# GpSimd splits the bias rows only after VectorE has made the one-hot tables of the edges

## The chip, the cores and the metric

The kernel runs on one core of one Trainium2 chip. The metric is the device time of one execution in microseconds (us). A core has five engines with queues of their own: TensorE (PE in the profile, PEld for its weight loads), VectorE (DVE), ScalarE (ACT), GpSimd (POOL) and SyncE (SP, which here issues most of the DMAs). They are ordered by semaphores alone.

## What is computed

Four graph layers over 64 nodes with 768 features and 1024 edges of 3 relations, each followed by a residual and a layer norm:

```python
x = layernorm(x + L0(x))   # 2 x (relational GCN, relu, gate over 64 queries)
x = layernorm(x + L1(x))   # GCN
x = layernorm(x + L2(x))   # 2 x relational graph attention
x = layernorm(x + L3(x))   # 2 x GCN

def rgcn(x, W_rel, W_root, bias, src, dst, etype):
    xr = einsum('ni,rio->rno', x, W_rel)
    msg = xr[etype, src]
    out = x @ W_root + bias
    for r in range(3):
        m = etype == r
        s = segment_sum(where(m[:, None], msg, 0.0), dst, n)
        c = segment_sum(m.astype(x.dtype), dst, n)
        out = out + s / maximum(c, 1.0)[:, None]
    return out
```

Nine bias vectors of 768 floats are inputs. They are given to the kernel as float32.

## The kernel before

**Edges as matrices.** The kernel never gathers along edges. It makes one-hot tables of the edges (128 partitions with 8 edges each): `hot_src` with 3 x 64 columns an edge (relation and source node) at L771, and `hot_dst` with 64 columns, written twice side by side, by the two instructions of L775. Eight bf16 matmuls (L1284) multiply the tables into a count matrix `M` of 64 x 192 in PSUM. From `M` VectorE makes degrees and the normalised adjacency (L782 to L801), PE turns it (L1295), and every graph layer multiplies with it.

**Biases.** A bias is added by a matmul of its own (L1123, L1160) into the PSUM bank of a layer. To keep float32 exactness with bf16 operands, each bias is split into three bf16 parts, stacked in the tile `biases` (3 x 32 rows, of which 9 each are used). GpSimd does this once: it clears `biases` (L579), waits for the nine bias rows from HBM, and then casts, subtracts and casts again (L581 to L586), each instruction waiting for the one before through `link`. The last two raise `biases_split`, and PE waits for 2 of it in front of the first layer's bias matmul.

**Start of the kernel.** The first 40 us prepare the gate of layer 0: `Wg` and the query embeddings arrive, PE turns them block by block (L1079), and ScalarE and VectorE copy each turned group from PSUM to the tiles `W` (L457). Groups are numbered, a group has three 128 x 128 blocks, and `group_on_act` says who copies which: of groups 8 to 13 VectorE has 11 and 13. Then PE multiplies the queries with the turned weights in eight units (`query_unit`, L1253). Each half of a unit is six records of L1253 in the trace. The order on each engine is written out by hand. On VectorE it is: group copies up to 7, the cast of the edge lists (L766, L768), L771, the two L775, group copies 11 and 13, the copy of unit 0 (L761), a further group, then the chain L782 to L801. On PE: transposes, half a unit, the transposes of groups 8 to 13, the other half of unit 0, then a wait until groups 8 to 13 are copied out (`wait_groups_out(pe, G_Q1)`), half of unit 1, the transposes of the next queries, a wait for the three tables, the counts, and so on to the mix of the nodes (L1269) and the first graph layer (L1105, 96 matmuls against four weight matrices of 2.3 MB).

**GpSimd.** Its stream makes constants for the first 10 us, then does the bias split, and is idle until the first gate. There it copies parts of the node terms into `stack` (L595) and makes 20 of the 32 products `prod = pre * qn` of that gate (L609); VectorE makes the other 12 (L905).

**Semaphores that matter here.** `hot_ready` counts the three tables (1 each from L771 and the two L775); before, only PE waits for it. `bias_loaded` counts 16 for each of nine row transfers, issued by ScalarE's queue. `pool_chain` orders GpSimd's own instructions. `blocks_ready` tells PE that the adjacency can be turned. The weight transfers are issued in order by SyncE: rel1_0 and rel1_1 at once, rel1_2 after the transposes of groups up to 13, root1 after the transposes of `Wg_h`.

Of the kernel before, what the change touches and what calls it, by code (L numbers as in the profile page):

```python
# [19 lines left out]
def gnn_kernel(nc: bass.Bass, a, out):  # L20
# [24 lines left out]
    SLOT = {key: s for key, s, _ in PLAN}  # L45
    PARTS = {key: n for key, _, n in PLAN}

    with ExitStack() as ctx:
# [3 lines left out]
        def sem(name):  # L52
            return ctx.enter_context(nc.semaphore(name))
# [119 lines left out]


        loaded = {key: [sem(f"{key}_{c}_loaded") for c in range(n)] for key, _, n in PLAN}
        Wg_q_rows = [sem(f"Wg_q_rows_{i}") for i in range(JC)]
        warm_ready = sem("warm_ready")
# [13 lines left out]
        hot_ready = sem("hot_ready")  # L191
# [345 lines left out]
        def _(pool):  # L537
            made = [0]

            def link(ins):  # L540

                made[0] += 1
                ins.then_inc(pool_chain, 1)
                pool.wait_ge(pool_chain, made[0])
# [32 lines left out]

            nb = len(BIASES)
            link(nc.gpsimd.memset(biases[:, :], 0.0))  # L579
            pool.wait_ge(bias_loaded, 16 * nb)  # L580
            link(nc.gpsimd.tensor_copy(biases[0:nb, :], bias[:, :]))  # L581
            link(nc.gpsimd.tensor_tensor(bias[:, :], bias[:, :], biases[0:nb, :], ALU.subtract))
# [1141 lines left out]
```

## Time and profile before

| | |
|---|---|
| median of 3 runs | 270.37 us (269.51 to 270.51) |
| profiled execution, its time | 270.35 us |
| its span, first to last instruction | 268.5 us |
| PE busy | 251.3 us (94%) |
| DVE busy | 158.6 us (59%) |
| ACT busy | 91.5 us (34%) |
| POOL busy | 86.3 us (32%) |
| granted TensorE clock | 1.000 |

How to read it: the profile is of one execution. Times in its rows count from the start of the span. A row of a timeline merges neighbouring instructions of one line and gives their start, their length from first start to last end, and their number (x6). What stands in square brackets is the idle time of the engine in front of it, and what ended it. `out<-in` names the tiles written and read.

### The profile page before, as it was taken

Reading aid. Unit: us, or ns where it says so; the run is one execution under the profiler, and the core shown is the slowest. Engines: PE = TensorE matmul, PEld = TensorE weight load, DVE = VectorE, ACT = ScalarE, POOL = GpSimd, SP = SyncE. Lnnn points to the kernel's source line nnn. Section 1 sums busy time; section 2 is a strip of 40 time slices with the busy share of each in tenths; the row PEclk is TensorE's granted clock in tenths of the full one; section 3 lists DMA queues with packets and bytes.
Section 4 is the critical chain, followed back from the end, with each engine's and each line's share of the span. In section 5 each row is a group of like instructions: output and inputs, shape, how many; then the busy total and the mean of one; then the engine's idle time right before and its main releaser. Section 6 shows DMA issues by size and latency. Waiting matters only on the chain.

```text
span 268.5 us, 4957 instructions
## 1 busy us (share of the span) xinstructions
PE 251.3 (94%) x2065; PEld 130.9 (49%) x2065; DVE 158.6 (59%) x283; ACT 91.5 (34%) x155; POOL 86.3 (32%) x76
## 2 busy tenths in 40 slices
PE   8899999999999999899999998889998988999994
PEld 4565874454435543356775222224573443435572
DVE  0866450015999999943015999996567267514422
ACT  2323340033657996412001667672302013013000
POOL 7790000003599999700000677870000000000000
PEclk9999999999999999999999999999999999999999
DMA  7999996996002967500699940003999636000001
GB/s 242 373 402 400 402 362 211 379 400 269 2 0 61 410 236 256 102 2 0 163 407 401 402 158 2 0 2 94 363 405 401 264 99 256 0 2 0 2 0 29
DMA packets 21895, 53.46 MB, mean 199 GB/s; under 512 B 4201, under 2 KB 4969, under 8 KB 21874
## 3 DMA queue, kind: packets, MB, share of 16 engines
q1 hardware_dynamic: 21184, 52.82, 53.6%
q10 hardware_dynamic: 690, 0.34, 0.5%
q8 instruction: 16, 0.26, 0.4%
q14 instruction: 5, 0.04, 0.0%
HBM read 52.17 MB, written 0.20 MB: 195 GB/s over the span
## 4 chain that ended last, share of the span: by engine, by line
PE 57%; POOL 17%; DVE 13%; issue 6%; ACT 4%; DMA 2%; SPq 0%; POOLq 0%; DVEq 0%; ACTq 0%
POOL prod L609 13%; PE ps L1137 12%; PE ps L1105 10%; PE ps L1253 6%; POOL W L609 4%; PE ps L1152 4%; PE ps L1079 3%; PE ps L1525 3%; PE ps L1605 3%; PE ps L1222 3%; DMA qn<-in_L_gnn_query_embs 2%; ACT pre L689 2%; DVE prod L905 2%; DVE pre L913 2%; PE ps L1343 2%
## 5 line engine op out<-in xcount | busy, mean ns | idle before, releaser
L609 POOL TENSOR_TENSOR prod<-pre,qn 128x768 f32<-128x768 f32 x28 | 56.0, 2023 | 11.5 <-ACT pre L689 11.5
L913 DVE TENSOR_TENSOR pre<-ps,qg 128x768 f32<-128x768 f32 x46 | 42.9, 950 | 2.0 <-PE ps L1329 0.9
L689 ACT ACTIVATE pre<-pre 128x768 f32<-128x768 f32 x46 | 38.7, 847 | 11.9 <-DVE pre L913 11.1
L1253 PE MATMUL ps<-W 128*128 128x384 f32 x96 | 34.7, 490 | 0.8 <-DVE W L457 0.5
L457 ACT COPY W<-ps 128x384 f32<-128x384 f32 x41 | 18.4, 483 | 39.4 <-PE ps L1079 39.2
L689 ACT ACTIVATE ps<-ps 128x768 f32<-128x768 f32 x18 | 14.2, 794 | 29.6 <-PE ps L1329 21.4
L1343 PE MATMUL ps<-prod,rsel 128*32 128x384 f32 x192 | 20.5, 496 | 3.4 <-POOL prod L609 2.7
L1253 PEld LDWEIGHTS ps<-W 128*128 128x128 f32 x96 | 17.3, 190 | 10.7 <-issue 2.0
L1137 PE MATMUL ps<-W,prod 128*64 128x256 f32 (+1 forms) x240 | 20.6, 328 | 0.0
L1079 PE MATMUL ps<-ident,W 128*128 128x128 f32 x144 | 19.7, 278 | 0.6 <-DMA W<-in_L_gnn_Wg 0.6
L1079 PEld LDWEIGHTS ps<-ident,W 128*128 128x128 f32 x144 | 16.9, 143 | 4.1 <-issue 1.3
L905 DVE TENSOR_TENSOR prod<-pre,qn 128x768 f32<-128x768 f32 x12 | 17.7, 1485 | 0.0
L1137 PEld LDWEIGHTS ps<-W,prod 128*64 128x64 f32 x240 | 15.1, 137 | 4.9 <-issue 0.5
L1222 PE MATMUL ps<-bsel 96*128 96x512 bf16 x62 | 16.9, 381 | 0.0
L1395 PE MATMUL ps<-stack,bsel 96*128 96x384 bf16 x64 | 15.8, 329 | 0.3 <-DVE pre L913 0.3
L1105 PE MATMUL ps<-W,prod 128*64 128x384 f32 x96 | 15.6, 486 | 0.0
L595 POOL COPY stack<-hi 32x384 bf16<-32x384 bf16 x2 | 1.2, 611 | 44.5 <-DVE hi L872 44.4
L457 DVE COPY W<-ps 128x384 f32<-128x384 f32 x15 | 8.3, 556 | 11.3 <-PE ps L1079 10.6
L1105 PE MATMUL ps<-W,nodeT 128*64 128x384 f32 x72 | 12.8, 492 | 0.0
L1137 PE MATMUL ps<-W,nodeT 128*64 128x256 f32 (+1 forms) x144 | 12.7, 328 | 0.0
L975 DVE CUSTOM_DVE_ANT_0 qn<-W,pre 128x768 bf16<-128x768 f32 x12 | 11.5, 955 | 1.7 <-DVE prod L975 1.7
L609 POOL TENSOR_TENSOR W<-pre,qn 128x768 f32<-128x768 f32 x6 | 10.9, 1824 | 3.2 <-ACT pre L689 3.2
(242 smaller groups left out, 333.8 us busy)
## 6 DMA issues: line engine op xcount, KB each, us to landing
W<-in_L_gnn_W SPq DMA_DIRECT2D x9, 2304.0 KB, 11.8
W<-in_L_gnn_W_rel SPq DMA_DIRECT2D x6, 2304.0 KB, 15.8
W<-in_L_gnn_W_root SPq DMA_DIRECT2D x2, 2304.0 KB, 9.5
W<-in_L_gnn_Wq SPq DMA_DIRECT2D x4, 1152.0 KB, 7.9
W<-in_L_gnn_Wg SPq DMA_DIRECT2D x3, 1152.0 KB, 13.2
qn<-in_L_gnn_query_embs SPq DMA_DIRECT2D x4, 384.0 KB, 10.2
W<-in_L_gnn_Wg SPq DMA_DIRECT2D x3, 384.0 KB, 3.9
W<-qg SPq DMA_DIRECT2D x2, 384.0 KB, 4.9
```

The costliest lines, as they stand in the source:

```text
L457: ins = nc.vector.tensor_copy(dst, src) if done is turned_out_v else nc.scalar.copy(dst, src)
L609: nc.gpsimd.tensor_tensor(prod_of(T), pre_of(T), qn[:, pair_and_node(t)[0], :], ALU.mult).then_inc(prod_p, 1)
L689: nc.scalar.activation(tile, tile, ACT.Sigmoid).then_inc(sig_ready, 1)
L905: nc.vector.tensor_tensor(by_half(prod_of(T)), src, by_half(qn[:, pair_and_node(T % TILES)[0], :]), ALU.mult).then_inc(prod_v, 1)
L913: nc.vector.tensor_tensor(dst, ring(T), by_half(qg[:, pair_and_node(T % TILES)[0], :]), ALU.add).then_inc(pre_ready, 1)
L1079: ins = nc.tensor.transpose(ps[:, group_bank(g), at:at + P], src, ident[:, :])
L1105: ins = nc.tensor.matmul(ps[c * N:(c + 1) * N, bank, 0:HD], T[:, j, col0 + h * N:col0 + (h + 1) * N], w[:, k, c * HD:(c + 1) * HD], start= ...
L1137: ins = nc.tensor.matmul(wide(bank)[c * N:(c + 1) * N, cols], T[:, j, col0 + h * N:col0 + (h + 1) * N], w[:, k, c * HD + cols.start:c * HD ...
L1222: nc.tensor.matmul(ps[:, bank, :], bsel[0:3 * GN, 0, :], bsel[0:3 * GN, 0:4, :].rearrange("p a b -> p (a b)"), start=True, stop=True, skip ...
L1253: ins = nc.tensor.matmul(ps[:, unit_bank(u), 0:HD], qT[:, k, p * P:(p + 1) * P], WgT_q[:, k, c * HD:(c + 1) * HD], start=(k == 0), stop=(k ...
L1343: ins = nc.tensor.matmul(ps[at:at + GN, ACC, 0:HD], rsel[:, s:s + GN], prod_of(T + g)[:, c * HD:(c + 1) * HD], start=first, stop=last, ski ...
L1395: ins = nc.tensor.matmul(ring(t)[:, c, :], bsel[0:3 * GN, t // 2, :], stack[:, c, t % 2, :], start=True, stop=True)
```

## The change

One line is added to GpSimd's stream: a wait for the third step of `hot_ready`, between the clearing of `biases` and the wait for the bias rows.

```diff
             nb = len(BIASES)
             link(nc.gpsimd.memset(biases[:, :], 0.0))
+            pool.wait_ge(hot_ready, 3)
             pool.wait_ge(bias_loaded, 16 * nb)
             link(nc.gpsimd.tensor_copy(biases[0:nb, :], bias[:, :]))
             link(nc.gpsimd.tensor_tensor(bias[:, :], bias[:, :], biases[0:nb, :], ALU.subtract))
```

No instruction that computes or transfers is added, removed or put on another engine.

## Rows read from the trace of the kernel before

**Rows 1.** The page: busy us of each engine, share of the span, number of instructions.

```profile
PE 251.3 (94%) x2065; PEld 130.9 (49%) x2065; DVE 158.6 (59%) x283; ACT 91.5 (34%) x155; POOL 86.3 (32%) x76
```

**Rows 2.** Chain of waits, 5 to 45 us: start us, us, what.

```profile
12.39 3.28 DVE prod L775 x2
16.61 0.14 issue
16.75 2.17 PE ps L1253 x6
...
41.47 15.48 PE ps L1105 x96
```

**Rows 3.** Timeline of DVE, 9 to 17 us.

```profile
10.63 1.76 DVE L771 TENSOR_TENSOR prod<-pre 128x1536 bf16<-128x1536 f32 x1
12.31 3.36 DVE L775 TENSOR_TENSOR prod<-pre 128x512 bf16<-128x512 f32 x2
15.60 1.01 DVE L457 COPY W<-ps 128x384 f32<-128x384 f32 x2
```

**Rows 4.** Timeline of POOL, 9 to 22 us.

```profile
11.94 1.13 POOL L581 CAST biases<-bias 9x768 bf16<-9x768 f32 x1 [1.57 <-DMA bias<-in_L_gnn_b]
13.15 1.97 POOL L582 TENSOR_TENSOR bias<-bias,biases 9x768 f32<-9x768 f32 x1
...
19.00 0.82 POOL L586 CAST biases<-bias 9x768 bf16<-9x768 f32 x1
```

**Rows 5.** The instructions of line L775, least, median and most ns.

```profile
L775 DVE TENSOR_TENSOR prod<-pre x2: 1309/1719/2129, 12.3 to 13.5; 128x512 bf16<-128x512 f32 x2
```

**Rows 6.** Timeline of PE, 12 to 41.5 us: start us, us, what.

```profile
12.10 2.18 PE L1079 MATMUL ps<-ident,W 128*128 128x128 f32 x18 [0.55 <-DMA W<-in_L_gnn_Wg]
14.12 2.10 PE L1253 MATMUL ps<-W 128*128 128x384 f32 x6
19.41 0.82 PE L1284 MATMUL ps<-prod 128*128 128x192 bf16 x8
...
27.84 0.60 PE L1295 MATMUL ps<-ident,prod 128*128 128x128 f32 x4
28.28 2.10 PE L1253 MATMUL ps<-W 128*128 128x384 f32 x6
30.22 1.47 PE L1079 MATMUL ps<-ident,qn 128*128 128x128 f32 x12
```

**Rows 7.** Waits of PE, 12 to 63 us: total us, times, longest.

```profile
PE ps L1253 <- DVE W L457: 0.5, 1, 0.5
```

**Rows 8.** Groups of DVE by line and shape: count, busy us, mean ns.

```profile
L761 DVE COPY qg<-ps 128x384 f32<-128x384 f32 x1 | 0.6, 558 | 2.0 <-PE ps L1253 2.0
L798 DVE TENSOR_TENSOR prod<-prod,ident 128x128 f32<-128x128 f32 x1 | 0.3, 293 | 0.0
```

**Rows 9.** Timeline of DVE: first and last of the chain of counts (13 rows).

```profile
20.28 0.36 DVE L782 COPY M<-ps 128x192 f32<-128x192 f32 x1
...
23.83 0.29 DVE L801 TENSOR_SCALAR prod<-prod,small 128x128 f32<-128x128 f32 x1
```

**Rows 10.** DMA issues, windows at 8 and at 16 us: KB, us to landing; timeline of SP.

```profile
W<-in_L_gnn_W_rel SPq DMA_DIRECT2D x1, 2304.0 KB, 21.4
6.07 3.77 SPq L478 DMA_DIRECT2D W<-in_L_gnn_W_rel  x1
...
W<-in_L_gnn_W_rel SPq DMA_DIRECT2D x1, 2304.0 KB, 23.8
15.41 5.71 SPq L478 DMA_DIRECT2D W<-in_L_gnn_W_rel  x1
```

**Rows 11.** Timeline of POOL: its first work after the bias split.

```profile
64.22 1.28 POOL L595 COPY stack<-hi 32x384 bf16<-32x384 bf16 x2 [44.40 <-DVE hi L872]
```

**Rows 12.** The products of the first gate, lines L905 and L609, ns.

```profile
L905 DVE TENSOR_TENSOR prod<-pre,qn x12: 946/1618/1635, 72.9 to 113.9; 128x768 f32<-128x768 f32 x12
L609 POOL TENSOR_TENSOR prod<-pre,qn x20: 1816/1834/2562, 70.1 to 110.5; 128x768 f32<-128x768 f32 x20
```

## The prediction

> **What bounds the kernel now.** I read the page first. The matrix engine (PE) is busy for 251.3 us, 94% of the span of 268.5 [rows 1], at a granted clock of 1.000, the upper of its two levels. So a change on GpSimd (POOL) can move the end only where PE, or the chain that feeds it, stands still for something that POOL sets. The second view is the chain of waits from 5 to 45 us [rows 2]. Up to 16.61 us it runs over VectorE (DVE), through the one-hot tables and two copies of turned weights; from 16.75 us on every piece belongs to PE. The reader is to see two things there: DVE carries the path just where the change acts, and the two instructions of L775 take 3.28 us on it although each makes only 512 elements a row.
>
> The third view is the timeline of DVE and POOL from 9 to 22 us [rows 3, 4]. L771 makes 1536 elements in 1.76 us; the two of L775 make 512 each and take 1309 and 2129 ns, the second from 13.5 on [rows 5]. Beside them POOL runs the cast L581 from 11.94 to 13.07 and the subtraction L582 from 13.15 to 15.12. The first L775 starts at 12.31 and ends at 13.62, 0.55 after the cast; the second ends at 15.67, 0.55 after the subtraction. Two equal instructions of unequal length, each ending the same time after a POOL instruction: DVE is held while POOL reads SBUF.
>
> The fourth view is PE's timeline and its waits [rows 6, 7]. Only one wait of PE in 12 to 63 us is for DVE: 0.53 us before the block at 16.75, for the weight copies (W, L457) that DVE makes behind the tables.
>
> **The change, part by part.** It adds one wait on POOL, in front of the wait for the bias rows. POOL's six instructions L581 to L586 then start when the second L775 is done. Nothing is removed, and POOL issues no DMA there, so no transfer is moved. Queued behind the wait on POOL are these six, then the stack copies L595. Who waits for them: PE, for the split biases in front of the first layer's matmuls at 41.47 [rows 2], and the first gate.
>
> Step 1, the tables alone. The price of an undisturbed table comes from two two-input DVE rows: 293 ns for 128 elements beside an idle POOL, and 1759 for 1536, of which only the last 0.45 us lie beside the cast [rows 3, 8]. That is (1759 - 293) / 1408 = 1.04 ns an element, so 512 elements cost 293 + 384 x 1.04 = 0.69 us. Successive DVE starts overlap by 0.08 (L771 starts at 10.63 and lasts 1.76, the next starts at 12.31). The tables then end at 12.31 + 0.61 + 0.69 = 13.6 instead of 15.67: DVE is 2.06 us earlier. From below this is bounded by 1309 ns for both, the shorter held row, which still ends them at 12.31 + 1.23 + 1.31 = 14.85.
>
> The Trainium skill bears on this (SBUF — State Buffer, section "Who interferes with whom"): a DVE instruction with two SBUF inputs and a GpSimd instruction that reads SBUF exclude each other, and whichever starts first blocks the other completely. The rows agree, with the two ends 0.55 us behind POOL's. By that rule the sum is the same as by the rows.
>
> Step 2, what is late next. DVE's two copies (groups 11 and 13 of the turned weights) were 1.01 us together at 15.60. They need PE's transposes of 12.10 to 14.28 [rows 6]. So the second can't end before 14.28 + 0.56 = 14.85 or so, whatever the tables do. The PE block in front (six records of L1253 at 14.12) takes 1.94 us to the next start when nothing holds it (28.28 to 30.22), so PE could go on at 14.12 + 1.94 = 16.06. The copies are out 1.2 us before that. PE gains 16.75 - 16.06 = **0.69 us**; by the wait row alone, which counts from a modelled end, 0.53 [rows 7]. The other 1.37 us of DVE's 2.06 become its idle time. Even with the bound of 14.85 for the tables, copies of 1.01 less the overlap of 0.07 and the 0.14 between copy and matmul [rows 2] give 15.93, so the full 0.69 stays. I take 0.69, since start to start doesn't lean on modelled ends; 0.53 is the low end and 0.76 the high (the block at 16.75 lasts 2.17, the others 2.10, if those 0.07 are an after-effect of the stall).
>
> Step 3, does it reach the end. PE works on without a wait until the first gate. What it needs on the way: the edge tables (L1284, 19.41), ready five us before; DVE's chain of counts L782 to L801, which ends at 24.12 [rows 9] and is used at 27.84, a margin of 3.7; and the weights. The transfers don't move with PE here. The first and the third of the first layer land at 27.5 and 39.2 (issues at 6.07 and 15.41 plus 21.4 and 23.8) [rows 10]. PE comes to them at 41.47 and 49.2 (96 records of L1105 in 15.48, a quarter for each matrix) [rows 2]. Margins of 14 and 10 us swallow 0.69. The fourth is triggered by PE's transposes, and all later ones are triggered by engines that move as well. The gates and layers behind are chains of engines that shift as a whole. So 0.69 arrives at the end.
>
> Step 4, where POOL's work goes. From 11.94 to 19.82 it is 7.88 us [rows 4]; started at 13.65, it ends at 21.5. The biases are read just ahead of 41.47 - 0.69 = 40.8, 19 us later, and POOL's next work was at 64.22 after 44.40 idle us [rows 11]. Cost: nothing, by that cover; without it, 1.7 us. But the tail now lies beside DVE's chain of counts, which starts at 20.28 - 0.69 = 19.6 and is 3.84 long. If every instruction of the chain excluded POOL's remaining 1.9 us, both would be done at 19.6 + 3.84 + 1.9 = 25.4, and PE wants the chain at 27.15. Covered with 1.8 us to spare.
>
> The rule of the Trainium skill named above speaks against the change at this place: the block works both ways, so a POOL instruction that meets a DVE instruction with two SBUF inputs waits as well. The worst case just worked out from the rows holds that too.
>
> **Sum.** The profiled execution took 270.35 us around a span of 268.5; the median of the runs shown is 270.37, so no correction is needed. 270.35 - 0.69 = **269.7 us**.
>
> **The rivals.**
> *The hold moves to DVE's copies.* POOL's cast now starts at 13.65, when DVE starts the copies that PE waits for. If copies from PSUM were held like the tables, both would wait for cast and subtraction, until 13.65 + 1.13 + 0.08 + 1.97 = 16.8, and PE would start at 16.8 + 0.94 + 0.14 = 17.9: 1.15 later than now, 271.5 us, slower. It decides from a hold of 1.2 us (gain gone) and 1.9 (slower). Against it: the pair at 15.60 took 1.01 together while POOL's split went on beside it, and the same copy in L761 took 558 ns beside an idle POOL [rows 3, 4, 8]. Chance 0.04.
> *Nothing comes of it.* Either the long L775 aren't POOL's doing (against it: 1309 and 2129 for equal work), or another wait, unseen in the trace because DVE was later, stands at 16.06, or the gates absorb it. 270.35 us. For it: a gain of a quarter of a per cent has little room to survive. Chance 0.15.
> *The first gate falls into another rhythm.* There DVE's products take 1618 ns at the median beside POOL's products, against 946 ns for the shortest: DVE's loses in nearly every round. Two that won would save 2 x (1.62 - 0.95) = 1.3, and with 0.69 give 268.3. Chance 0.07. The other way, a POOL product held costs 2.56 - 1.83 = 0.73 [rows 12]; three more give 270.35 - 0.69 + 2.2 = 271.9, slower. It would need DVE to issue first, and POOL runs there almost without gaps. Chance 0.06.
>
> **How the numbers follow.** Forecast 0.68, nothing 0.15, copies held 0.04, gate faster 0.07, gate slower 0.06. The predicted time is the first's. The forecast's own bounds are 269.6 to 269.8, and the three runs of before spread from 269.51 to 270.51, so about half a us each way belongs to a median. Forecast and nothing together span 269.0 to 270.7 with that; this is the range, and it leaves out most of the other cases. About 0.5% (1.35 us) is what a measurement of this kernel can tell from no change. Faster by that needs the fast gate and a bit of luck: 0.09. Slower needs the slow gate or the held copies with more: 0.07. The rest, 0.84, lies within.
>
> **What would show each step.** In the profile after: both L775 at about 0.69 us and equal; L581 starting at 13.6 to 13.8; DVE's copy of group 13 out by 15.0; PE's wait of 0.53 gone and its block at 16.06; L1295 and the block of L1105 earlier by 0.69 (27.15 and 40.8); POOL's split done by 21.5 to 22.5; the span 267.8. Wrong would be: L775 above 1.3 us, copies above 0.6, a new wait of PE between 16 and 28 us, or a shift at 41 us that isn't there at 116.

## The result

The changed kernel takes **269.69 us** (median of 22 executions, 269.39 to 269.96), against 270.32 us for the kernel before in as many (269.51 to 270.55). The ratio is 0.9981, with a 95% interval of 0.9975 to 0.9987: 0.51 us faster, between 0.35 and 0.68. The forecast was 269.7 with a gain of 0.69. The two medians stand 0.63 apart; why the ratio says less comes further down, with the single times.

In the changed kernel the lines behind the new wait have numbers one higher (L776 was L775, L582 was L581). Header and busy times of the page, where VectorE's busy time is 2.3 us shorter and PE's is the same:

```profile
span 268.0 us, 4957 instructions
PE 251.1 (94%) x2065; PEld 131.2 (49%) x2065; DVE 156.3 (58%) x283; ACT 91.6 (34%) x155; POOL 85.3 (32%) x76
```

The line L776, the one with the tables of the destinations (least, median, most ns), to be held beside [rows 5]:

```profile
L776 DVE TENSOR_TENSOR prod<-pre x2: 684/684/684, 12.3 to 12.9; 128x512 bf16<-128x512 f32 x2
...
  POOL biases L582: 3.4, 1
```

The timeline of DVE, against [rows 3] and [rows 9], and that of POOL, against [rows 4] and [rows 11]:

```profile
10.64 1.76 DVE L772 TENSOR_TENSOR prod<-pre 128x1536 bf16<-128x1536 f32 x1
12.32 1.28 DVE L776 TENSOR_TENSOR prod<-pre 128x512 bf16<-128x512 f32 x2
13.92 1.21 DVE L457 COPY W<-ps 128x384 f32<-128x384 f32 x2 [0.32 <-PE ps L1080]
...
19.77 0.36 DVE L783 COPY M<-ps 128x192 f32<-128x192 f32 x1
...
23.32 0.28 DVE L802 TENSOR_SCALAR prod<-prod,small 128x128 f32<-128x128 f32 x1
```

```profile
13.73 0.81 POOL L582 CAST biases<-bias 9x768 bf16<-9x768 f32 x1 [3.36 <-DVE prod L776]
14.63 1.63 POOL L583 TENSOR_TENSOR bias<-bias,biases 9x768 f32<-9x768 f32 x1
...
19.79 0.82 POOL L587 CAST biases<-bias 9x768 bf16<-9x768 f32 x1
63.71 1.28 POOL L596 COPY stack<-hi 32x384 bf16<-32x384 bf16 x2 [43.10 <-DVE hi L873]
```

Both tables take 684 ns and end at 13.60 instead of 15.67. DVE now waits 0.32 us for PE in front of its copies, where it was late before. The chain of counts lasts 3.83 us, as before (3.84). POOL's own instructions are shorter too: the cast 0.81 instead of 1.13 us, the subtraction 1.63 instead of 1.97. The split ends at 20.61, only 0.8 us later than before although it starts 1.8 later.

PE's timeline, against [rows 6]:

```profile
12.36 2.18 PE L1080 MATMUL ps<-ident,W 128*128 128x128 f32 x18 [0.43 <-DMA W<-in_L_gnn_Wg]
14.38 4.04 PE L1254 MATMUL ps<-W 128*128 128x384 f32 x12
18.25 0.82 PE L1080 MATMUL ps<-ident,qn 128*128 128x128 f32 x6
18.90 0.82 PE L1285 MATMUL ps<-prod 128*128 128x192 bf16 x8
...
27.33 0.60 PE L1296 MATMUL ps<-ident,prod 128*128 128x128 f32 x4
```

The two blocks of six records that stood 2.63 us apart, start to start, are now one row of twelve. The whole stretch starts later, though: the second part of Wg landed 0.26 us later in this execution (12.36 instead of 12.10), which the change doesn't touch. From these transposes to L1285 it is 18.90 - 12.36 = 6.54 us, and was 19.41 - 12.10 = 7.31. The stall was worth 0.77 us; less the 0.26 of the later landing, 0.51 is left. This 0.51 is found again at L1296 (27.33 for 27.84) and at the end of the span (268.0 for 268.5). The chain of waits now begins with that transfer where it had DVE's tables [rows 2]:

```profile
2.58 9.73 DMA W<-in_L_gnn_Wg
12.31 0.04 issue
12.36 2.18 PE ps L1080 x18
14.54 3.87 PE ps L1254 x12
```

### The profile page after: what moved, and what is told of

Its sections match the earlier page's. It is cut to its first block, busy times and chain, and to the rows that moved or that the text cites. A ratio compares the mean times of both kernels' runs of the same rounds, so it can differ in the third digit from the quotient of the medians.

```text
span 268.0 us, 4957 instructions
## 1 busy us (share of the span) xinstructions
PE 251.1 (94%) x2065; PEld 131.2 (49%) x2065; DVE 156.3 (58%) x283; ACT 91.6 (34%) x155; POOL 85.3 (32%) x76
## 4 chain that ended last, share of the span: by engine, by line
PE 58%; POOL 17%; DVE 10%; issue 6%; DMA 4%; ACT 4%; SPq 1%; POOLq 0%; DVEq 0%; ACTq 0%
POOL prod L610 13%; PE ps L1138 12%; PE ps L1106 10%; PE ps L1254 7%; POOL W L610 4%; PE ps L1080 4%; PE ps L1153 4%; DMA W<-in_L_gnn_Wg 4%; PE ps L1526 3%; PE ps L1606 3%; PE ps L1223 3%; ACT pre L690 2%; DVE prod L906 2%; DVE pre L914 2%; PE ps L1344 2%
## 5 line engine op out<-in xcount | busy, mean ns | idle before, releaser
L690 ACT ACTIVATE pre<-pre 128x768 f32<-128x768 f32 x46 | 38.7, 847 | 11.9 <-DVE pre L914 11.1
L1138 PE MATMUL ps<-W,prod 128*64 128x256 f32 (+1 forms) x240 | 20.6, 328 | 0.0
L1396 PE MATMUL ps<-stack,bsel 96*128 96x384 bf16 x64 | 15.8, 329 | 0.3 <-DVE pre L914 0.3
```

Of the source, the lines that this page charges most:

```text
L690: nc.scalar.activation(tile, tile, ACT.Sigmoid).then_inc(sig_ready, 1)
L1138: ins = nc.tensor.matmul(wide(bank)[c * N:(c + 1) * N, cols], T[:, j, col0 + h * N:col0 + (h + 1) * N], w[:, k, c * HD + cols.start:c * HD ...
L1396: ins = nc.tensor.matmul(ring(t)[:, c, :], bsel[0:3 * GN, t // 2, :], stack[:, c, t % 2, :], start=True, stop=True)
```

## The experiments

The theory: POOL's reads of SBUF hold DVE's two-input tables (a hold: an instruction of one engine waits, already issued, until one of the other engine is done); behind them lie 1.2 us of slack; a shift of PE reaches the end one to one. The rivals: another cause of the long tables, a price of the split's new place, and a shift that gets lost.

### Only write, don't read

```diff
             pool.wait_ge(bias_loaded, 16 * nb)
+            for _ in range(2):
+                link(nc.gpsimd.memset(stack[:, :, :, :], 0.0))
```

> The kernel before without the new wait, but with two memsets of the tile stack (96 x 1536 bf16, write only) between the bias rows' arrival and the bias split. POOL is busy beside the tables from 11.9 to about 14.9 us, but reads nothing there; the split follows from 14.9 on. Theory (it is POOL's reading of SBUF that holds a VectorE instruction with two SBUF inputs): both L775 take 0.69 us, PE has no stall at 16 us, 269.7. Rival (any work of POOL holds VectorE): L775 take over 1.2 us each or together over 3, PE stalls, 270.3 or more.

Measured: 269.80 us in the median of 10 executions, the slowest 269.92; ratio to before 0.9985 (0.9975 to 0.9994). The timelines of POOL and DVE of this kernel:

```profile
12.27 2.81 POOL L582 MEMSET stack<- 96x1536 bf16 x2 [1.91 <-DMA bias<-in_L_gnn_b]
...
21.20 0.82 POOL L588 CAST biases<-bias 9x768 bf16<-9x768 f32 x1
```

```profile
12.31 1.28 DVE L777 TENSOR_TENSOR prod<-pre 128x512 bf16<-128x512 f32 x2
...
20.85 0.32 DVE L789 TENSOR_SCALAR small<-small 128x3 f32<-128x3 f32 x1
...
21.42 0.81 DVE L795 TENSOR_TENSOR prod<-M,small 64x192 f32<-64x192 f32 x1
```

POOL writes from before the first table to after the second, and both take 682 ns. It is the reading that holds them, and the rival is out. The same trace also shows the hold in a place where nobody pays for it. The split now lasts until 22 us, and a two-input step of the chain of counts beside its last cast takes 0.81 us instead of 0.35. The chain ends 0.6 us later than it would, and PE, which wants it at 27, doesn't notice. So without the new wait, but with no read beside the tables, the time is that of the changed kernel within the noise (269.80 for 269.69).

### Wait for one table instead of three

```diff
-            pool.wait_ge(hot_ready, 3)
+            pool.wait_ge(hot_ready, 1)
```

> The changed kernel, but POOL waits for the first table (L771) only, so its cast L582 comes free at about 12.4 us, while the first of the two instructions L776 is running or about to. Theory (one excludes the other for a whole instruction, and whoever starts first wins): the tables of L776 no longer both wait for POOL; at least the first takes 0.69 us and POOL's cast waits for it. The second meets the cast: it is held by at most its 0.81 us, and the tables end by 14.5. PE's stall stays away, since VectorE has 1.2 us of slack, and the time is that of the changed kernel, 269.7. Rival (only the end of all tables helps, because POOL's subtraction starts within them): the second takes over 2 us, the tables end after 15.3, PE stalls as before, 270.3.

Measured: 269.67 us (10 executions, 269.49 to 269.98); ratio 0.9987 (0.9977 to 0.9996). Line L776 of this kernel, then the timelines of DVE and of POOL:

```profile
L776 DVE TENSOR_TENSOR prod<-pre x2: 684/998/1311, 12.3 to 12.9; 128x512 bf16<-128x512 f32 x2
```

```profile
12.30 1.91 DVE L776 TENSOR_TENSOR prod<-pre 128x512 bf16<-128x512 f32 x2
14.14 1.01 DVE L457 COPY W<-ps 128x384 f32<-128x384 f32 x2
```

```profile
12.51 1.15 POOL L582 CAST biases<-bias 9x768 bf16<-9x768 f32 x1 [2.16 <-DVE prod L772]
13.74 1.97 POOL L583 TENSOR_TENSOR bias<-bias,biases 9x768 f32<-9x768 f32 x1
```

This resolves the hold into single turns. The first table starts at 12.30 before the cast and takes its 684 ns. The cast, started at 12.51, takes 1.15 us, which is 0.34 over its 0.81, and ends at 13.66. The second table takes 1311 ns and ends at 14.21, 0.55 after it; the subtraction is lengthened in its turn, by 0.34. Each waits for the other's instruction in flight, and neither is passed over. The one hold that is left costs DVE 0.63 us, and that lies in its slack. The two copies behind it ran beside the subtraction in 1.01 us without a gap, so copies from PSUM aren't held.

So what hurt in the kernel before was that POOL's cast came first, at 11.94 for 12.31: then DVE waits twice, once for the cast and once for the longer subtraction. That cast was itself held by L771. It ended at 13.07, 0.68 us behind the end of L771 (12.39), just as here it ended 0.68 behind the end of the first table (13.66 for 12.98).

### A longer read

The kernel before, and in front of its subtraction another one of 9 x 1536 elements:

```diff
             link(nc.gpsimd.tensor_copy(biases[0:nb, :], bias[:, :]))
+            link(nc.gpsimd.tensor_tensor(stack[0:nb, :, :, :].rearrange(...),
+                                         bias[:, :].unsqueeze(1).to_broadcast([nb, 2, D]),
+                                         biases[0:nb, :].unsqueeze(1).to_broadcast([nb, 2, D]), ALU.subtract))
```

> The kernel before, with one POOL subtraction of twice the length (9 x 1536 elements into stack, about 3.3 us against 1.97) put in front of L582, so that it is what the second L775 meets at 13.5 us. Theory: the second table ends 0.55 us after this instruction, at about 17.0 instead of 15.67; PE stalls 1.3 us longer, and the whole kernel takes 1.3 us more than before: 271.6. Rival (the hold has a length of its own, or later work absorbs it): the table ends at 15.7 as before, or PE's end doesn't move, 270.3.

Measured: 269.68, 271.79, 271.80, 271.85 and 273.49 us. The profile is of the last of these: the line of the tables, the longer read in POOL's timeline, and the stalled block in PE's.

```profile
L778 DVE TENSOR_TENSOR prod<-pre x2: 1310/2445/3580, 12.3 to 13.6; 128x512 bf16<-128x512 f32 x2
```

```profile
13.17 3.42 POOL L582 TENSOR_TENSOR stack<-bias,biases 9x1536 bf16<-9x1536 f32 x1
```

```profile
18.22 3.11 PE L1256 MATMUL ps<-W 128*128 128x384 f32 x6 [2.06 <-DVE W L457]
```

The second table lasts 3580 ns and ends 0.55 us behind POOL's end at 16.59: the hold is as long as what POOL reads. The three middle times are 1.45 above the 270.35 of the kernel before, as the table is 1.45 longer than 2129 ns. That settles size and path. The other two times showed two things that the forecast had not had, the next two parts.

### The two groups of times

269.68 is the time of the changed kernel, reached by a kernel that is built to be slower. It has companions in the kernel before: of its 99 executions that were run beside the changed kernel and the experiments, 32 took 269.46 to 269.99, 62 took 270.29 to 270.55, and only 5 lie between. None of the changed kernel's 22 is above 269.96. The explanation to test: whether the cast or the first table comes first depends on when the nine bias rows land, and that varies from one execution to the next. The wait for one table, above, puts the cast behind the table always, and all its 10 executions were under 270. The high group needs both holds: of the 83 executions of the changed kernel and of six experiments that exclude at least one (one table, write only, split at 29, one more table, the later memset, the held loads), none took more than 270.10.

Two more try the race itself, with the kernel before. The first delays the cast by a short memset:

```diff
             pool.wait_ge(bias_loaded, 16 * nb)
+            link(nc.gpsimd.memset(stack[:, 0, 0, :], 0.0))
```

> The kernel before, without the new wait, with one small memset (write only, about 0.4 us) between the arrival of the bias rows and the cast L582, so that the cast starts at about 12.4 to 12.8 us, after the first table has started at 12.3. Theory (the executions of the kernel before that take 269.6 are those in which the bias rows land after the first table's start; then only one table is held, by one cast, and VectorE's slack swallows it): the tables end at about 14.2, PE has no stall, and all executions are near 269.7, with none of the 270.35 that most executions of before show. Rival (the two groups of times in the kernel before have another source, such as the landing of Wg): times at 270.3 remain.

Measured: eight executions from 269.60 to 269.88, three at 270.23, 270.37 and 270.39. The profile is of a low one, here POOL's timeline and DVE's:

```profile
12.02 0.41 POOL L581 MEMSET stack<- 96x384 bf16 x1 [1.66 <-DMA bias<-in_L_gnn_b]
12.49 1.17 POOL L582 CAST biases<-bias 9x768 bf16<-9x768 f32 x1
```

```profile
12.30 1.91 DVE L776 TENSOR_TENSOR prod<-pre 128x512 bf16<-128x512 f32 x2
```

The cast starts 0.19 us behind the table and the pattern is that of the wait for one table. The expectation that no high time would remain was wrong: 3 of 11 are left, where the kernel before has 62 of 99. How they arise is not shown. The rows landed between 11.87 and 12.27 in the traces where POOL waited for them; the earliest would put this cast at 12.34, still behind the table, and no trace of a high execution was taken. The second moves the landing:

```diff
-            for h in range(2):
-                act.dma_start(xa[...], a["x"][...]).then_inc(x_loaded, 16)
             for i, name in enumerate(BIASES):
                 act.dma_start(bias[i:i + 1, :], ...).then_inc(bias_loaded, 16)
+            for h in range(2):
+                act.dma_start(xa[...], a["x"][...]).then_inc(x_loaded, 16)
```

> The kernel before with ScalarE's transfers of the nine bias rows issued ahead of the two of x, so that the rows land about a microsecond earlier. Theory of the race: now the cast always comes before the first table, both tables are held in every execution, and the time is 270.3 or above in all of them, with nothing near 269.6. If the cast comes so early that it lies wholly beside L771, the subtraction meets the first table and one hold is enough: the tables then end near 15. Rival (other source of the two groups): the same mixture as before, about one execution in three under 270.0.

Measured: 11 executions from 269.86 to 270.33, median 270.08, in no groups. The expectation failed, and the trace says on what. The timelines of DVE, POOL and PE:

```profile
9.51 0.17 DVE L766 CAST pre<-eidx 128x24 f32<-128x24 int32 x1
...
11.59 3.38 DVE L775 TENSOR_TENSOR prod<-pre 128x512 bf16<-128x512 f32 x2
14.89 1.01 DVE L457 COPY W<-ps 128x384 f32<-128x384 f32 x2
```

```profile
10.45 1.90 POOL L581 CAST biases<-bias 9x768 bf16<-9x768 f32 x1
```

```profile
12.59 2.18 PE L1079 MATMUL ps<-ident,W 128*128 128x128 f32 x18 [1.15 <-DMA W<-in_L_gnn_Wg]
14.61 4.04 PE L1253 MATMUL ps<-W 128*128 128x384 f32 x12
```

The cast came 1.5 us earlier, but it didn't get done beside L771: that one has two inputs in SBUF too and held it, for 1.90 us instead of 0.81, until 12.35, again 0.68 behind L771's end. So both tables are held (3.38 us as before), but they start 0.7 us earlier: DVE's small cast L766 got in front of POOL's memset L579 and took 0.17 us, where it took 0.78 behind it. Wg lands at 12.59 instead of 12.10, so PE also comes later. Between the two the stall is gone. This kernel isn't a clean test of the race, since it moved three things at once. What it shows is that two holds alone cost nothing. They need the late start of the tables as well: the copies here are out at 15.90, in time even for the block at 16.06 that a Wg at 12.10 allows.

That leaves a second explanation of the two groups, which no run separates from the first. The start of L771 is not one number either. It is 10.57 to 10.66 in eleven of the thirteen traces and 9.91 and 9.92 in two, where DVE's small cast came ahead of the memset: here, and in the kernel with five more tables below, whose early group is 3 of its 10. With that start the kernel before would have its copies out by 15.9 whichever comes first, in time for PE (an estimate, from the copies here). And the four traces that show when the bias rows landed have them before 12.31, the late start of the first table. So the 32 low executions in 99 may be those with the early start; the 8 of 11 above speak for the order of cast and table as well. No low execution of the kernel before was profiled, and the source of its groups stays open.

### The slack

One and five more tables on DVE, ahead of the two (`n` is 1 or 5):

```diff
+            for _ in range(n):
+                link(nc.vector.tensor_tensor(hot_dst[:, :, 0:N], ..., ALU.is_equal))
             for h in range(2):
                 nc.vector.tensor_tensor(hot_dst[:, :, h * N:(h + 1) * N], ...
```

> The changed kernel, with one more instruction like L776 (the first half of hot_dst written once more, with a wait behind it, about 0.75 us) on VectorE ahead of the two. Theory: VectorE's weight copies are out 1.2 us ahead of PE in the changed kernel, so 0.75 more on VectorE doesn't reach PE: no stall before its block at 16.3, 269.7. Rival (VectorE still sets the path and every piece of its 2.06 us counts): 0.7 slower, 270.4.

Measured: 269.62 us (269.48 to 269.81); ratio 0.9975 (0.9966 to 0.9984). In PE's timeline the blocks are one row, without a stall, and in DVE's the copies are out at 15.27, 1.0 us ahead of the second block (14.34 + 1.94). In the changed kernel it was 1.2; the rest of the 0.72 us filled DVE's idle time in front of the copies:

```profile
13.05 1.29 DVE L780 TENSOR_TENSOR prod<-pre 128x512 bf16<-128x512 f32 x2
14.26 1.01 DVE L457 COPY W<-ps 128x384 f32<-128x384 f32 x2
```

```profile
14.34 4.04 PE L1258 MATMUL ps<-W 128*128 128x384 f32 x12
```

> The same with five more instructions (about 3.7 us). Theory: 1.2 us of them are slack and the other 2.5 stall PE before its block, and reach the end one to one: 269.7 + 2.5 = 272.2. Rival A (all of it counts): 273.4. Rival B (the gates or the transfers behind absorb part of any shift): clearly under 272.2, down to 270.5.

Measured: 271.89 us, in groups again: three at 271.15 to 271.21, five at 271.86 to 272.07, two at 273.61 and 273.78. The profile is of the first group; DVE's timeline and PE's:

```profile
9.52 0.17 DVE L767 CAST pre<-eidx 128x24 f32<-128x24 int32 x1
```

```profile
17.60 2.17 PE L1258 MATMUL ps<-W 128*128 128x384 f32 x6 [1.55 <-DVE W L457]
```

There the small cast came ahead of the memset, so the tables started at 9.92 instead of 10.64. PE's block starts at 17.60 instead of 13.95 + 1.94 = 15.89, 1.71 late, and the span is 269.4: 1.7 above the 267.7 of the kernel further down whose Wg landed about as early (used at 12.01 for 11.93 here) and which has no stall. A start of 10.64 would add 0.7 and give the middle group. The top group has a mean granted clock of 0.992 and 0.993, against 0.996 to 1.000 in the others; it wasn't profiled, but a stall followed by a lower clock looks so in the last run of the next part. The five tables are 3.62 us (11.60 to 15.22). The middle group is 2.2 above the changed kernel, so about 1.4 us of them was slack, and beyond it the stall arrives one to one. The expectation had put the slack at 1.2: that is how early the copies are, and the tables in front of them have the 1.37 that the prediction left over.

The other side of the same thing is to take the memset away from that cast:

```diff
-            link(nc.gpsimd.memset(biases[:, :], 0.0))
             pool.wait_ge(hot_ready, 3)
+            link(nc.gpsimd.memset(biases[:, :], 0.0))
```

> The changed kernel, with the memset of biases (L579) put behind the new wait as well, so that POOL is idle from about 9.6 to 13.7 us. VectorE's cast L767 took 0.41 to 0.78 us beside that memset. Theory: the cast takes under 0.3 us and the tables end up to 0.3 us earlier, but VectorE has slack, so the time is 269.7, the same. Rival (what is taken off VectorE there still counts): 269.4 or less.

Measured: 269.68 us (269.55 to 269.95), the changed kernel's time. The cast took 0.17 us. The tables ended at 13.53, earlier by 0.07 only, since the group copy in front of them ended later in this execution. It is in the slack either way.

### The split's place

```diff
-            pool.wait_ge(hot_ready, 3)
+            pool.wait_ge(adj_ready, 2)
```

> The changed kernel, but POOL waits for the turned adjacency (the copies of L805 and L806, 28.3 to 28.8 us) instead of the tables. The bias split runs from about 28.8 to 36 us, all of it behind the chain of counts, and is done 4 us ahead of PE's bias matmul at 40.6. Theory (the split's place costs nothing between 13.7 and 33 us, and its tail beside the chain of counts costs nothing either): 269.7, with the same chain of counts within 0.1 us. Rival (the split beside the chain of counts or the copies holds something on the path in the changed kernel): this one is faster than 269.7 by 0.3 or more; or it is slower by as much, because the split now meets VectorE's weight copies at 30 to 36 us.

Measured: 269.58 us (269.43 to 270.04), ratio 0.9986 (0.9975 to 0.9997). The split ran from 28.57 to 35.47. Neither the chain of counts nor the copies pay for its place in the changed kernel.

And so late that the cover is gone:

```diff
-            pool.wait_ge(hot_ready, 3)
+            pool.wait_ge(mix_out_v, JC)
```

> The changed kernel, but POOL waits for VectorE's three copies of the mixed nodes (L845, done at about 39 us). The bias split then takes until about 46 us, while PE wants it at 40.6. This takes the cover away. Theory: PE stands still for 5.6 us there; the weights have landed by then, so nothing absorbs it: 269.7 + 5.6 = 275.3. Rival (PE's wait moves transfers that are waited for later, so that more or less than the stall arrives): over 276 or under 274.5.

Measured: 277.23 us (four executions, 276.91 to 278.14), 1.9 more than expected. That is in the range of the rival, but later transfers are not the reason: of the 7.7 us between the profiled executions, 7.6 are already there at the transposes behind the first layer (63.97 for 56.37). The stall is 5.47 us, as worked out, and then PE's clock falls. The timeline of PE, and a table of stretches (their length, the busy time of PE, PEld, DVE, ACT and POOL, then the granted clock, DMA share and GB/s):

```profile
45.70 0.53 PE L1124 MATMUL ps<-biases,i 96*64 96x384 bf16 x2 [5.47 <-POOL biases L587]
```

```profile
40.20:45.70 5.50, 0.03 (x1) 0.03 (x1) 0.56 (x1) 0.00 (x0) 5.09 (x5) 0.84 0.50 197
45.70:47.00 1.30, 1.29 (x6) 0.77 (x8) 0.00 (x0) 0.00 (x0) 0.00 (x0) 0.50 0.05 13
47.00:49.00 2.00, 2.00 (x8) 0.79 (x6) 0.00 (x0) 0.00 (x0) 0.00 (x0) 0.50 0.00 0
49.00:51.00 2.00, 2.00 (x10) 0.83 (x8) 0.00 (x0) 0.00 (x0) 0.00 (x0) 0.55 0.00 0
```

After 5.5 us without work the clock is at 0.50, the lower of its levels (1.2 GHz), until about 50.8. From the bias matmuls to the next transposes PE took 63.97 - 45.70 = 18.3 us, and 56.37 - 40.61 = 15.8 in the changed kernel: 2.5 us for the clock in this execution. The median is 7.5 above the changed kernel's, 5.5 for the stall and 2.0 for the clock. The highest execution of the longer read, 273.49, is the same at a shorter stall:

```profile
16.10:18.20 2.10, 0.07 (x1) 0.01 (x1) 2.10 (x4) 0.00 (x0) 2.02 (x2) 1.00 1.04 404
18.20:20.00 1.80, 1.78 (x5) 1.10 (x6) 0.34 (x1) 0.00 (x0) 1.65 (x3) 0.81 1.01 394
20.00:22.00 2.00, 2.00 (x8) 1.29 (x7) 0.00 (x0) 0.00 (x0) 1.94 (x2) 0.50 1.05 409
22.00:24.00 2.00, 2.00 (x14) 1.66 (x13) 1.09 (x3) 0.48 (x1) 0.93 (x2) 0.82 1.02 396
```

There it fell behind 2.06 us of standing still, with PE at work again, and cost 273.49 - 271.8 = 1.7 us. The three middle executions of that kernel don't show such a time. In the kernel before, with 0.53 us, and in the profiled one with five more tables, with 1.55, it stayed at 1.00.

### What bounds it next

The changed kernel's chain begins with Wg. One attempt to have it land earlier:

```diff
+            sp.wait_ge(turned, 1)
             for p in PAIRS[1:]:
                 load_queries(p)
```

> The changed kernel, and SyncE issues the last three query loads and all that follow only when PE has turned its first group (about 5.8 us instead of 3.1), since the changed kernel's chain now starts with the landing of the second part of Wg at 12.3 us. Theory: with less traffic beside them the first query block and that part of Wg land about 1 us earlier, PE's two waits for transfers (0.4 and 0.4 us) go, VectorE's tables follow its earlier group copies, and the kernel takes 269.0 to 269.3. Rival (the later loads come too late and stall PE at the queries of 17.9 us or at Wg_h, or the landing doesn't depend on the other traffic): 269.7 or more.

Measured: 269.65 us (269.58 to 270.10), the changed kernel's time. The part of Wg was used from 12.17 on, within what other executions show (11.9 to 12.6), although the loads behind it were issued from 6.30 us on instead of 3.07. The rival holds: its landing doesn't depend on how early they are issued. What it does depend on stays open. No kernel here is faster than the changed one by more than the noise (269.58 to 269.68 in five medians, for 269.69).

## Why the prediction was right

*The tables.* 0.69 us each was worked out from two other rows; 684 ns was measured. The ends 0.55 us behind POOL's, taken as the sign of a hold, were one: reads of a chosen length moved them, writes didn't. The rule of the Trainium skill (SBUF — State Buffer, "Who interferes with whom") holds in every trace here, in both its parts, the blocking by whoever is first (1.15 us for POOL's cast behind a table, 1311 ns for a table behind the cast) and the freedom of DVE beside a POOL instruction that only writes (2.81 us of memsets, 682 ns a table).

*What is late next.* PE's own block, as forecast. The margin of the copies is 14.38 + 1.94 - 15.13 = 1.2 us, and the runs with more tables bear it out. The block itself went on at 16.32 and not at 16.06, by the later Wg. The gain of the stall itself was 0.77, at the top of the stated 0.53 to 0.76: the 0.07 by which the stalled block was longer did belong to the stall.

*Reaching the end.* 0.51 us at 27, and 0.5 at the end of the span. The one-to-one passage also holds for +1.7 us (five more tables) and for the 1.45 of the longer read. For stalls of 2.06 and 5.47 us the clock added a price of its own, in one execution of the longer read and in the split at 40.

*The split's place.* It cost nothing, and the last instruction ended at 20.6 where 21.5 was forecast, because POOL also got rid of its share of the holds: L581, L582 and L583 had been 0.32 to 0.35 us longer each. That was in the rule that was cited against the change, and not in the sum. The worst case beside the chain of counts didn't come: the chain took 3.83 us.

*Without cover.* The prediction priced it at 1.7 us, POOL's later start alone. The run at 40 us shows how such a price is made up: the part of the split that PE has to wait for, 5.5 us there, and 2.0 for the clock.

*The rivals.* Held copies: none, 1.01 us for two beside a subtraction. (By the prediction's own sums a hold of 1.2 us would begin to eat the gain and one of 1.9 would take all of it; it called the first "gain gone" and the second "slower".) Another rhythm of the first gate: DVE's products there stayed at 944/1621/1630 ns and POOL's at 1815/1837/2548, against [rows 12]. Nothing comes of it: true of a third of the executions of the kernel before, which took the changed kernel's time already.

*Where it was right by less than it seems.* The forecast took the one profiled execution for the kernel. In the comparison of the result 16 of the kernel before's 22 executions lay in the upper group. The means of the two sets are 270.17 and 269.66, 0.51 apart, which is what the ratio says. The medians differ by 0.63 because the median of the kernel before lies in the upper group. The profile happened to be of that group. 0.69 was the gain against it, not against all. That the forecast met the median to 0.01 us is luck: the two profiled executions are 0.55 apart, and the landing of Wg alone moved PE's start by 0.26 between them. The range of 269.0 to 270.7 was also a little off by its own terms, which give 269.1 to 270.85.

## What to carry to other kernels

Two equal instructions of unequal length on VectorE, each ending the same time behind a GpSimd instruction that reads SBUF, were a hold here; give GpSimd a wait only if its work has cover, and price the gain by the engine that is late next, not by the hold. Here 2.06 us taken off VectorE were worth 0.77. Look at the single times as well as the median: two tight groups 0.7 us apart said that something in the kernel's order isn't fixed, and a wait that fixed the order of cast and tables took the slow group away. One profile shows one of the groups only.

## What the hardware showed beside

- Two engines that hold each other took turns instruction by instruction. With the table first, both tables together took 14.21 - 12.30 = 1.91 us; with the cast first they took 3.36. A held table ended 0.55 us behind GpSimd's instruction, for reads of 1.13 to 3.42 us; GpSimd's held cast ended 0.67 to 0.68 us behind VectorE's instruction, in five traces.
- A cast of 24 elements on VectorE takes 0.17 us ahead of GpSimd's memset and up to 0.78 behind its start, ending when the memset ends (10.4 us). The memset of 1.4 us didn't hold a two-input table; this one holds a cast. This decides the start of the tables (9.92 or 10.64).
- TensorE's clock fell to its lower level (granted 0.50) behind a stall of 2.06 us in one profiled execution, and behind 5.47 us in another; behind 0.53 and 1.55 us it stayed at 1.00. It cost 1.7 and 2.5 us, the first nearly as much as its stall. Three more executions of the first kernel have times that fit the same stall without such a cost.
